# Attention masks built by TensorE in PSUM, and the third bf16 part of the weighed rows on GpSimd

## The reference, cut to what matters

```
for i in range(4):
    Q = _ln(h @ Wq[i], gq[i], bq[i]);  K = _ln(h @ Wk[i], gk[i], bk[i])
    qi = Q[src];  kj = K[dst]
    score = (qi * kj).sum(-1) + 0.1 * (edge_attr * qi[:, :40]).sum(-1) + logm[dst]
    smax  = segment_max(score, src, num_segments=N)
    es    = exp(minimum(score - smax[src], 20.0))
    denom = segment_sum(es, src, num_segments=N)
    alpha = es / (denom[src] + 1e-10)
    aggi  = segment_sum(alpha[:, None] * (h[dst] @ Wm[i]), src, num_segments=N)
    z = leaky_relu(concat([h, aggi]) @ Wu[i], 0.01)
    h = _ln(h + z, go[i], bo[i])
```

## Time and profile before

| | |
|---|---|
| median of three runs | 15027.07 us |
| the profiled execution: its own time, its span | 15085.92 us, 15084.2 us |
| busy: TensorE, VectorE, ScalarE, GpSimd | 75%, 81%, 56%, 50% of the span |
| granted TensorE clock, mean of the span | 0.587 of full |
| strips of `attend` | 1040 |
| largest group that the change touches | L1006, 1178.5 us on ScalarE |

### The profile page before, as it was taken

One profiled execution on the slowest core, in us unless ns is written; L12 is line 12 of the kernel. 1 busy time (PEld: TensorE's weight loads), 2 busy tenths in 40 slices (PEclk: granted clock), 3 DMA queues, 4 the chain that ended last, 5 costly groups with the idle time before them and its releaser, 6 DMA issues. The chain is left out here.

```text
span 15084.2 us, 633523 instructions
## 1 busy us (share of the span) xinstructions
PE 11381.7 (75%) x194575; PEld 9646.2 (64%) x194575; DVE 12169.1 (81%) x29602; ACT 8505.6 (56%) x28744; POOL 7505.2 (50%) x9217
## 2 busy tenths in 40 slices
PE   3677777764666688879888888888886667676576
PEld 3455555543566687768777877777776666676566
DVE  7566666655789889988998889988998778699986
ACT  0444444434567678867887688867885202067630
POOL 3455555543445455536554555545552454565445
PEclk5555555555775675558555955586555657585585
DMA  9322222246589677748775777757776856579856
GB/s 377 92 62 63 63 64 64 63 53 110 193 276 284 212 267 189 189 130 301 187 189 149 280 191 187 188 209 220 185 185 191 270 168 200 149 280 281 224 200 169
DMA packets 3519407, 2773.01 MB, mean 184 GB/s; under 512 B 2341177, under 2 KB 3123128, under 8 KB 3519018
## 3 DMA queue, kind: packets, MB, share of 16 engines
q1 hardware_dynamic: 2793946, 1087.59, 28.4%
q0 software_dynamic: 236192, 860.68, 19.4%
q10 hardware_dynamic: 489008, 821.78, 14.7%
HBM read 1656.63 MB, written 1112.41 MB: 184 GB/s over the span
## 5 line engine op out<-in xcount | busy, mean ns | idle before, releaser
L1327 PE MATMUL ps<-arena 128*128 128x49 bf16 x56160 | 2729.6, 218 | 1021.9 <-DVE arena L1838 494.6
L1327 PEld LDWEIGHTS ps<-arena 128*128 128x128 fp8e4 x56160 | 2456.4, 119 | 1353.3 <-issue 1351.2
L1294 PE MATMUL ps<-block_tables,arena 128*128 128x98 bf16 (+2 forms) x56160 | 2451.0, 201 | 558.6 <-DVE arena L1808 273.6
L1294 PEld LDWEIGHTS ps<-block_tables,arena 128*128 128x128 bf16 (+1 forms) x56160 | 2218.7, 99 | 791.5 <-issue 413.9
L777 POOL COPY block_tables<-arena 128x294 bf16 (+2 forms) x2340 | 1427.4, 610 | 2198.7 <-PE ps L1294 1321.6
L738 POOL DMA_INDIRECT edge_records<-arena x1563 | 1635.6, 1046 | 1329.1 <-ACT arena L893 887.6
L970 ACT ACTIVATE arena<-ps 128x392 f32<-128x392 f32 (+1 forms) x3900 | 1710.4, 480 | 1023.1 <-PE ps L1294 611.2
L761 POOL DMA_INDIRECT arena<-chunk_layer_rows,map_a x1040 | 1066.0, 1025 | 2094.1 <-ACT arena L1034 2005.4
L1034 ACT ACTIVATE arena<-arena,small 128x49 f32<-128x49 f32 x8320 | 1996.9, 323 | 104.5 <-ACT small L1026 6.0
L1808 DVE TENSOR_SCALAR arena<-arena,iota_row 128x1024 bf16<-128x1024 uint8 x2080 | 1565.3, 753 | 111.3 <-PE ps L1294 50.9
L1822 DVE TENSOR_TENSOR arena<-arena 128x392 f32<-128x392 f32 x2340 | 1358.0, 580 | 355.2 <-PE ps L1327 309.5
(11 more groups left out here) (332 smaller groups left out, 20298.4 us busy)
## 6 DMA issues: line engine op xcount, KB each, us to landing
chunk_layer_rows<-arena ACTq DMA_DIRECT2D x1040, 392.0 KB, 3.3
arena<-node_hot_a SPq DMA_DIRECT2D x1820, 128.0 KB
arena<-edge_hot_a SPq DMA_DIRECT2D x1560, 128.0 KB
chunk_gated<-arena ACTq DMA_DIRECT2D x520, 324.0 KB, 2.6
arena<-edge_records SPq DMA_DIRECT2D x1040, 160.0 KB
chunk_rows<-arena ACTq DMA_DIRECT2D x780, 196.0 KB, 1.9
arena<-edge_records SPq DMA_DIRECT2D x520, 196.0 KB
arena<-edge_hot_b SPq DMA_DIRECT2D x780, 128.0 KB
```

The lines of the kernel that those rows point to most:

```text
L1294: last = pe.matmul(psv[:, 2 * r + j // tpb, (j % tpb) * w:(j % tpb + 1) * w], hot[:, s, j * P:(j + 1) * P], bt4[:, s, i, 0:w], start=i == ...
L1327: last = pe.matmul(to[s % 2], he4j[:, s % 4, j, :], low_part(i, s, j), start=j == 0 and i == 0, stop=j == C8 - 1 and i == 2)
```

## The change

Two steps move to other engines, both in `attend` only.

1. The mask is no longer made by ScalarE. TensorE writes it into PSUM ahead of the spread scores (`mask_s`, lag 1, between `pick_query` and `turn_s`): for each of two banks one matmul of 512 columns with `big_off` (row 0 is -1e30) against ones, and one of 512 columns with `big_on` (1e30 on the diagonal) against the fp8 one-hots. `spread_s` then adds to what stands there (start=False). `mask_s` takes over the wait for the last `peak`. `peak` becomes a plain reduction of 1024 elements from PSUM. `masks`, `hn4`, `at["not"]` and SyncE's wait for it are gone.
2. `twice` leaves VectorE. GpSimd makes x2 (`thirds`) at the end of iteration k of `collect`, for strip k - 8, after waiting for x1 of that strip.

```
@@ collect and GpSimd's layer
-            def collect(tab, w_row, used, base, w, picked, picked_base, more=None):
+            def collect(tab, w_row, used, base, w, picked, picked_base, more=None, last=None):
                 def after(k):
                     if 3 <= k < NS + 3:
                         source_block(w, picked, picked_base, k - 3)
                     if more is not None and 4 <= k < NS + 4:
                         more(k - 4)
+                    if last is not None and 8 <= k:
+                        last(k - 8)
                 gather(tab, w_row, map_a, used, base, after)
-                for k in range(NS, NS + 4):
+                for k in range(NS, NS + (4 if last is None else 8)):
                     after(k)
...
+            def thirds(l, k):
+                pool.wait_ge(x1_made, (l + 1) * NS + k + 1)
+                pool.tensor_tensor(x2[:, k % 2], x1[:, k % 2], x1h[:, k % 2, :, :, 1], ALU.subtract).then_inc(x2_made, 1)
...
-                collect(ed_l, ROWL, at["ph"], l * NS, WK, at["q"], l * NS, lambda k: keys(l, k))
+                collect(ed_l, ROWL, at["ph"], l * NS, WK, at["q"], l * NS, lambda k: keys(l, k), lambda k: thirds(l, k))
@@ ScalarE
-                def masks(k, s):
...
-                    act.activation(hn4[:, s % 4, :], hs4[:, s % 4, :], ACT.Identity, bias=neg_big[:, 0:1], scale=BIG).then_inc(at["not"], 1)
-                walk(nc, act, NS, [(2, weights), (2, weigh), (1, READ), (0, masks), (1, corrected, True), (0, turn), (1, kept, True)], (ACT_ENGINE, blk_a))
+                walk(nc, act, NS, [(2, weights), (2, weigh), (1, READ), (1, corrected, True), (0, turn), (1, kept, True)], (ACT_ENGINE, blk_a))
@@ TensorE
+                def mask_s(k, s):
+                    again(pe, at["gm"], base, k, 1)
+                    for h in range(2):
+                        pe.matmul(psv[:, 4 + h, :], big_off, all_ones, start=True, stop=False, skip_group_check=True)
+                        pe.matmul(psv[:, 4 + h, :], big_on, hs4[:, s % 4, h * 512:(h + 1) * 512], start=False, stop=False, skip_group_check=True)
                 def spread_s(k, s):
                     r = s % 2
                     pe.wait_ge(at["ev"], base + k + 1)
-                    again(pe, at["gm"], base, k, 1)
                     for j in range(C8):
                         last = pe.matmul(psv[:, 4 + j // 4, (j % 4) * P:(j % 4 + 1) * P], sel[:, j * P:(j + 1) * P],
-                                         s_turn[:, r * P:(r + 1) * P], start=True, stop=True)
+                                         s_turn[:, r * P:(r + 1) * P], start=False, stop=True, skip_group_check=True)
...
-                walk(nc, pe, NS, [add_up(l + 1, l + 1, ps_att, parts, 4), (0, pick_query), (1, turn_s), (2, pick_max), (1, spread_s)])
+                walk(nc, pe, NS, [add_up(l + 1, l + 1, ps_att, parts, 4), (0, pick_query), (1, mask_s), (1, turn_s), (2, pick_max), (1, spread_s)])
@@ VectorE
-                    hold(dve, "dve", (at["bc"], base + k + 1), (at["not"], base + k + 1))
-                    dve.tensor_tensor_reduce(out=junk[:, :], in0=ps[:, 4 * 512:6 * 512], in1=hn4[:, s % 4, :],
-                                             scale=1.0, scalar=-BIG, op0=ALU.add, op1=ALU.max, accum_out=gm[:, r:r + 1]).then_inc(at["gm"], 1)
+                    hold(dve, "dve", (at["bc"], base + k + 1))
+                    dve.tensor_reduce(gm[:, r:r + 1], ps[:, 4 * 512:6 * 512], AX.X, ALU.max).then_inc(at["gm"], 1)
...
-                                   (2, once), (3, READ), (2, twice), (3, add_raised, True)], (DVE_ENGINE, blk_a))
+                                   (2, once), (3, READ), (3, add_raised, True)], (DVE_ENGINE, blk_a))
```

More of the change, by code:

```diff
@@ L434, in build @@
         at = {n: sem("att_" + n) for n in (
-            "q", "keys", "not", "prod", "red", "mid", "tr", "ev", "bc", "gm", "max", "low", "cor",
+            "q", "keys", "prod", "red", "mid", "tr", "ev", "bc", "gm", "max", "low", "cor",
             "sub", "exp", "ph")}
@@ L679, in layer @@
                 spread(l + 1, row_b)
-                walk(nc, sp, NS, [(0, load_node_hots(l * 2 + 3, l)), (0, load_edges(0, R, at["keys"], l * NS)), (2, load_edge_hots(hot_ea, l + 1))])
+                walk(nc, sp, NS, [(0, load_node_hots(l * 2 + 3)), (0, load_edges(0, R, at["keys"], l * NS)), (2, load_edge_hots(hot_ea, l + 1))])
             with sp.Fori(0, L - 1) as l:
@@ L1925, in add_raised @@
                     dve.scalar_tensor_tensor(o, o, cor[:, s % 4:s % 4 + 1], ps_att[s % 2], ALU.mult, ALU.add).then_inc(acc_done, 1)
-                once, twice = lower(hs_no, weighed, there)
+                once, _ = lower(hs_no, weighed, there)
                 walk(nc, dve, NS, [(2, shifted), (0, products), (1, READ), (1, peak), (0, reduced), (1, raised, True), (0, middles), (1, low),
-                                   (2, once), (3, READ), (2, twice), (3, add_raised, True)], (DVE_ENGINE, blk_a))
+                                   (2, once), (3, READ), (3, add_raised, True)], (DVE_ENGINE, blk_a))
                 dve.wait_ge(acc_done, (hs_no + 1) * NS)
```

21 lines of the change are left out of this document (10 added, 11 removed).

## The result

The changed kernel takes 15,815.06 us (median of 4 runs, 15,807.88 to 15,830.75), the kernel before 15,031.11 us on the same chip (4 runs, 15,020.17 to 15,038.46). The ratio is 1.052, with a 95% interval of 1.0507 to 1.0533: 784 us slower. The forecast was 15,610 us, by the case of a mixed clock. The profiled execution took 15,807.88 us, its span is 15,805.9 us.

What follows compares the result with a forecast made beforehand. VectorE bounded the kernel at 4.386 us a strip; the new ring at mixed clock gives 4.95. (4.95 - 4.386) x 1040 = +590 us on 15,027 makes 15,617, stated as 15,610 us; range 14,950 to 15,950.

Steps and rivals of the forecast that it cites:

- the case of a mixed clock: Likeliest case in `attend`: clock a third full, two thirds half, 4.95 us a strip, +590 us; chance 0.50.
- The ring: In `attend`, waits from `shifted` through `weigh`, gather, `thirds`, TensorE and `pick_max`, carrying two strips: 10.48 us half clock, 8.76 full.
- The hand-over from GpSimd to TensorE: Between the end of `thirds` and `add_up` on TensorE, a part of the two-strip ring, estimated at 0.06 us.
- The clock's mix: TensorE's clock in `attend`, taken from a `spread` walk's row: a third of the time full, two thirds half.
- the ring's two sums: The two-strip ring in `attend`: 10.48 us at half clock (5.24 a strip), 8.76 at full (4.38 a strip).
- The wait for x2: TensorE's idle time before L1327 in `attend`, to be put down to GpSimd's `thirds` (L820), about 0.98 us each.
- The gather's wait: GpSimd's wait for `weigh` before the gather in `attend`, to shrink from 2.0 to about 1 us or a little more.
- VectorE's reduction: `peak` in `attend`, changed from two inputs to a plain reduction: 1224 to 1194 ns, 30 ns less.
- Half clock throughout: Rival in `attend`: ring and TensorE's own work both 5.24 to 5.4 us a strip, +890 to +1050 us; chance 0.17.
- full clock throughout: Rival in `attend`: the ring at full clock gives 4.38 us a strip, about 15,020 us in all; chance 0.25.
- VectorE's bound: Rival in `attend`: VectorE remains the bound, relieved of 0.65 us, 3.73 us a strip, 14,350 us; chance 0.08.
- The price of `thirds`: `thirds` on GpSimd in `attend`: 0.98 us in proportion to `keys`; the skill's ratio was said to give some 0.14 more.

Runs made afterwards that it cites:

- e3: The changed kernel with `thirds` on GpSimd moved ahead of the query block's copy and `keys`, masks on TensorE; 1.0076 of the kernel before.
- e7: The kernel before (masks on ScalarE) with `thirds` on GpSimd, ahead of the query block's copy and `keys`; 0.9866 of the kernel before.
- e2: The kernel before (masks on ScalarE) with only `thirds` moved to GpSimd, behind `keys`; 1.0172 of the kernel before.
- e4: The changed kernel plus two useless matmuls of 448 columns a strip on TensorE behind `spread_s`; 1.0331 of the kernel before.
- e9: The changed kernel with `thirds` on GpSimd moved ahead of the gather's issue, masks on TensorE; 0.988 of the kernel before.
- e10: The kernel before (masks on ScalarE) with `thirds` on GpSimd, ahead of the gather's issue; 0.9868 of the kernel before.
- e11: As e10, with a strip's reduction on VectorE put behind the scores of the next strip; 1.0563 of the kernel before.

## Why the prediction was right, and where it was off

- **The ring** through `thirds` was there, and its parts were nearly right: from `shifted` to the end of `thirds` 5.55 us against 5.81, `thirds` itself 0.84 against 0.98, masks 1.55 us, most of them at half clock (6006.94 to 6008.49), against 1.75, and 0.96 at full (6001.31 to 6002.27) against 0.90. The hand-over from GpSimd to TensorE was sized 0.06 and takes 0.24 (from 6004.72 to 6004.96) and 0.36 (from 14.88 to the next `add_up` at 6015.24). What shows it isn't this sum but e3 and e7: moving this one instruction forward on GpSimd, with every engine's work unchanged, gave 676 us (the change to e3) and 457 us (e2 to e7), and the trace has x2 1.2 us sooner in both.
- **The clock's mix** is the step that was mis-sized. I took one third full and two thirds half, and weighed the ring's two sums with it: 4.95 us. Measured is 0.83, the mirror image, which weighed the same way gives 4.67. The strip takes 5.12. Right sign and a fair number, because two errors offset: more full clock than I assumed, but the half-clock stretches fall on the part of TensorE's work that stands in the ring. e4 shows the size of the clock's part, 287 us or more.
- **The wait for x2** was to be about 0.98 us in each strip. It is 1.41 us in the piece shown and comes before about every second strip, 0.66 us a strip in the mean: two chains of strips pass TensorE in turn, and only one of them finds it idle.
- **A wait left out.** `mask_s` waits for the last reduction: 0.47 us in the fast strip, 170.6 us in the whole run. In the same chain of strips, the other one than I summed above, `keys` also waits 0.41 us for its edge records. I had neither.
- **The gather's wait** for `weigh` was to shrink from 2.0 to about 1 us. It is 2.06 us a strip (201.9 us in 98 strips): the strip grew by about as much as GpSimd's work. A wrong reading, with no part in the sum.
- **VectorE's reduction** was to take 30 ns less than the form with the mask; both take 1,225. Its idle time grew to 1.63 us a strip, as expected, and above all before L1922.
- **The rivals.** Half clock throughout did not come. Nor did full clock throughout; it came nearest in another kernel, e9 (0.98 in its last stage, 4.02 us a strip). VectorE's bound, 3.73 us, was reached by no order; e10 shows what is next to VectorE, 4.16 us.
- **The price of `thirds`.** By the ratio 1.96 of the Trainium skill (GPSIMD Engine Reference, section 3.1, Elementwise), measured there on 2048 elements, it is an estimate of 1.23 us, counted from the 625 ns that the same work took on VectorE. That is 0.25 us over my 0.98, not the 0.14 that the prediction gives, and 0.12 us a strip. `thirds` takes 838 ns, 1.34 times as long as on VectorE, so the measurement decides against the figure. That GpSimd is the slower engine for it is right, and it made no difference in e7, where it is hidden.
- **The swinging clock.** In the stretches above the clock is 1.00 and 0.50 in turn, 0.83 in the mean, and the half clock follows TensorE's pause of 1.41 us for x2. The Trainium skill (TensorE: Matmul & The Clock Gate, Part 1, HAM oscillation) has a loop whose pauses for DMA return throttled again in every turn; the traces agree that a pause which returns can do this, here a wait for another engine.

What stays open: how much of the 5.12 us is each ring's. The trace after shows two chains of strips, one held by TensorE's half clock and one with the waits for the reduction and the edge records, and no run separates these two. Nor does any run change the clock alone: with it changed TensorE's work or the place of `thirds`.

## What to carry to other kernels

When a step moves to an idle engine, its place in that engine's program counts for more than the engine's free time: follow who waits for the result and who must run before it can start, and count how many turns the loop so closed carries. Issued behind two instructions that nobody was waiting for, the same 0.84 us cost 1.7%; ahead of them it gained 1.3%. And price two halves of a change together if they lie on the same ring: apart they cost 0.55% and 1.7%, together 5.2%.

## What the runs showed of the hardware

- What stands behind a short instruction on VectorE has a price. The load of a block number takes 0.31 us there. Ahead of the reduction, from start to start, it cost 0.77 us with only an instruction of 8 elements running beside it (e11), and 0.85 us with `products` (0.56 us) running beside it (e10). The recorded length of the 8-element instruction then reads 638 ns in place of 167, so a recorded length isn't always the instruction's own work.
- The instruction right behind a reduction of 1024 elements that reads its result first waited 0.27 us (e11); with another in between it didn't wait (e10).
- From the end of an instruction on GpSimd to the matmul that waits for it, 0.24 us is the shortest of all runs with `thirds`, and 0.29 the mean in e2, where TensorE waits for it in 100 of 108 strips.
- Added matmuls can shorten a stage: two of 448 columns a strip, with no use, took 287 us off `attend` as the clock rose from 0.83 to 0.91. Removed ones can lengthen it: two of 512 columns fewer, clock 0.92 to 0.76, 146 us more by the traces and 56 by the medians.
- TensorE at 94% busy in `attend` (471.40 of 500 us, e7) kept the half clock throughout, and 82% busy in e3 (412.07 of 500 us) had 0.91: here the busy share does not tell the clock.
- A reduction of 1024 elements from PSUM takes 1,225 ns, the same as the two-input form that added a mask in the same pass.
- Chips differ outside the stages studied: all but `attend` took 9,408 to 9,440 us on one and 10,500 to 10,562 on the others, for kernels that differ in `attend` alone; the kernel before took 13,926 us on the one and 15,031 to 15,076 on the others. No kernel was traced on both kinds. The 13,926 less 9,408 to 9,440 leaves 4,486 to 4,518 us for `attend` there, and 4,570 less the 55 to 59 us by which that execution was slow is near it, which is why stage times are compared between chips here and whole times only as ratios.
